# Attention with half-array scores and a three-step lead, and feed-forward stages with normalising on GpSimd and wide passes

## The reference

```python
def attend(q, k, v):                      # 16 heads of 16
    return softmax(q @ k.T / 4) @ v       # over 256 keys
x = x + lora_linear(attend(q(ln(x)), k(ctx), v(ctx)))   # W + 2 A B for q, k, v, o, with biases
x = x + sqrt((ln(x) @ cos(theta + tn))**2 + (ln(x) @ sin(phi + pn))**2)
x = x + linear(attend(rope(q(ln(x))), rope(k(ctx)), v(ctx)))
h = gelu(quant16(ln(x)) @ quant8(W_in) + b_in)          # 256 to 1024 features
x = x + quant16(h) @ quant8(W_out) + b_out
```

## Time and profile before

| What | Value |
|---|---|
| median of 3 runs | 2490.02 us (2481.99 to 2492.55) |
| span of the profiled execution | 2491.9 us; no other time of that execution is given |
| busy in the span | PE 78%, PE weight load 63%, DVE 70%, ACT 53%, POOL 32% |
| granted clock, mean | 0.880 |
| DMA | 333.54 MB, mean 134 GB/s |

### The profile page before, as it was taken

The page is one execution under the profiler, slowest core; times in us unless marked ns, Lnnn a source line. Parts: engine busy times, 40 slices in busy tenths (PEclk is TensorE's granted clock), DMA queues, the critical chain, the costliest instruction groups (busy, mean ns, idle before and its releaser), DMA issues. The chain is left out here.

```text
span 2491.9 us, 47293 instructions
## 1 busy us (share of the span) xinstructions
PE 1955.9 (78%) x14240; PEld 1576.1 (63%) x14240; DVE 1747.3 (70%) x3674; ACT 1316.8 (53%) x2381; POOL 797.0 (32%) x866
## 2 busy tenths in 40 slices
PE   1689999999999679277788777887777775786687
PEld 0567777777777467255666666666666663665676
DVE  6567778877877378465667767767666665676788
ACT  0255666656655378144444444444444443786676
POOL 3012222222222200423333333333333332221787
PEclk9899999999999689578888888888888877898899
DMA  5576887888878100356665656666666661356565
GB/s 164 107 157 145 169 172 162 166 169 166 170 161 165 53 3 0 76 104 122 123 120 116 117 109 116 119 112 118 111 118 122 121 118 54 135 220 252 196 242 186
DMA packets 259781, 333.54 MB, mean 134 GB/s; under 512 B 29152, under 2 KB 237184, under 8 KB 251520
## 3 DMA queue, kind: packets, MB, share of 16 engines
q1 hardware_dynamic: 233088, 277.00, 49.4%
q0 software_dynamic: 26624, 55.67, 9.6%
HBM read 185.70 MB, written 144.70 MB: 133 GB/s over the span
## 5 line engine op out<-in xcount | busy, mean ns | idle before, releaser
L610 DVE TENSOR_REDUCE L_negm<-L_s_bank 128x2 f32<-128x512 f32 x1024 | 684.4, 684 | 363.2 <-PE L_s_bank L418 360.7
L475 ACT ACTIVATE L_prob<-L_t_bank 128x512 f32<-128x512 f32 x1024 | 598.9, 598 | 631.8 <-PE L_t_bank L429 625.7
L418 PE MATMUL L_s_bank<-L_kst,L_qst 96*128 96x256 f32 x2048 | 526.1, 343 | 236.5 <-DMA L_kst<-k_scratch 176.7
L418 PEld LDWEIGHTS L_s_bank<-L_kst,L_qst 96*128 96x128 f32 x2048 | 355.4, 216 | 363.0 <-issue 142.0
L429 PE MATMUL L_t_bank<-L_qst,L_kst 98*128 98x256 f32 x2048 | 460.6, 311 | 18.3 <-ACT L_prob L475 15.2
L429 PEld LDWEIGHTS L_t_bank<-L_qst,L_kst 98*128 98x128 f32 x2048 | 361.7, 217 | 33.3 <-ACT L_prob L475 30.0
L339 PE MATMUL L_o_bank<-L_prob,L_vext 128*32 128x256 f32 x4096 | 301.1, 415 | 2.7 <-ACT L_prob L475 2.7
L1289 PE MATMUL G_acc<-G_w_out,G_hhl 128*128 128x256 f32 x1024 | 140.4, 291 | 59.4 <-DVE G_hhl L1259 59.1
L259 POOL DMA_DIRECT2D L_den<-o_scratch x64 | 35.5, 554 | 452.2 <-DMA o_scratch<-L_osb 452.2
L1289 PEld LDWEIGHTS G_acc<-G_w_out,G_hhl 128*128 128x128 f32 x1024 | 127.9, 192 | 72.1 <-DVE G_hhl L1259 37.5
L339 PEld LDWEIGHTS L_o_bank<-L_prob,L_vext 128*32 128x32 f32 x4096 | 112.5, 115 | 92.6 <-issue 18.8
(11 more groups left out here) (172 smaller groups left out, 3257.2 us busy)
## 6 DMA issues: line engine op xcount, KB each, us to landing
L_qst<-q_scratch SPq DMA_DIRECT2D x384, 128.0 KB, 5.0
L_kst<-k_scratch SPq DMA_DIRECT2D x384, 128.0 KB, 6.4
q_scratch<-L_qhl SPq DMA_DIRECT2D x64, 512.0 KB, 3.0
k_scratch<-L_khl SPq DMA_DIRECT2D x64, 512.0 KB, 3.2
o_scratch<-L_osb POOLq DMA_DIRECT2D x128, 256.0 KB, 4.8
hidden_scratch<-G_hid SPq DMA_DIRECT2D x32, 1024.0 KB, 3.9
G_hid<-hidden_scratch SPq DMA_DIRECT2D x32, 1024.0 KB, 7.4
L_ctx_in<-in_ctx SPq DMA_DIRECT2D x64, 256.0 KB, 3.2
```

Source lines behind the costliest of these rows:

```text
L418: mm = pe.matmul(s_bank[k % 2][:, j, :], qst[1 - q][0:96, h, P * qt:P * (qt + 1)], kst[1 - q][0:96, h, :], start=True, stop=True)
L475: act.activation(prob[g % 2][:, k % 2, 2 * (k // 2 % 2):2 * (k // 2 % 2) + 2, :], t_bank[k % 2][:, :, :], ACT.Exp, scale=HD ** -0.5).then_ ...
L610: dve.tensor_reduce(negm[:, t, 2 * pair:2 * pair + 2, qt], s_bank[k % 2][:, :, :], AX.X, ALU.max, negate=True).then_inc(sem["dve_s"], 1)
```

## The change

In both attentions a head's stack has 48 rows (50 with the maxima) and lies in rows 0 to 49 or 64 to 113. A slot holds one head position of both feature halves; the half of the rows alternates with the batch, so that the scores of batch i+1 and the transposed scores of batch i lie in opposite halves, and their four matmuls are issued in turn. A batch is normalised by GpSimd and projected three steps before its exponentials (q, k) or two (v). ScalarE copies projections and values out of PSUM, GpSimd splits q and k; the rotation takes its swapped copy by DMA between partitions (`rotated`, two DMAs of 64 partitions) and is done by GpSimd (`times`, a product); q and k are stored in pieces of 4 KB and stacked in pieces of 2 KB. The bias of v is folded into that of the output. The context's split transpose is stored by layer 0 and loaded by layer 1. Outputs (`eo`, heads in 17 columns) stay in SBUF: denominators, `merge` and the spread of the reciprocals (`rb`) are DMAs on SP's queue, and GpSimd multiplies. `weighted(n, half)` is the product of exponentials and v for eight heads. The memsets of the stacks go.

In the feed-forward stages GpSimd normalises, and in `cos_sin_ffn` it also adds to x; maxima in `quantised_in` are taken over 1024 columns; `quantised_out` works on half chunks of 2048 columns, with three load buffers, and GpSimd and VectorE share the scaling back. All loops are written out. Below, added lines without their outer indent.

```diff
-    for c, part in enumerate(order):
-        sp.dma_start(dst[HD * c:HD * (c + 1), HT * t:HT * (t + 1), :].bitcast(F32),
-                     dram[part, t].rearrange("(h d) q -> d h q", d=HD)).then_inc(done, 16)
+def stack(n, half):
+    u = n % 2 ^ half
+    for st, dram, high in ((kst[n % 2], k_dram[n % 2], KH), (qst[n % 2], q_dram[n % 2], QH)):
+        part = dram.rearrange("(j d) c t q -> j d c (t q)", d=HD)[HJ * u:HJ * (u + 1)]
+        sp.dma_start(st[64 * u:64 * u + 2 * HD, :, :, :].bitcast(F32), part.rearrange("j d c n -> (d c) j n")).then_inc(sem[f"stack{half}"], 16)
+        sp.dma_start(st[64 * u + 2 * HD:64 * u + ROWS, :, :, :].bitcast(F32),
+                     part[:, :, high, :].rearrange("j d n -> d j n")).then_inc(sem[f"stack{half}"], 16)
...
+def step(i):
+    if on(i + 1):
+        after(sp, sem["pe_t"], 16 * i)
+        stack(i + 1, 1)
+    if on(i):
+        maxima(i, 1)
+    if on(i + 2):
+        after(sp, sem["stack1"], 64 * (i + 1))
+        sp.wait_ge(sem["pool_k"], i + 3)
+        store(khl, k_dram[i % 2], sem["k_store"])
+        sp.wait_ge(sem["pool_q"], i + 3)
+        store(qhl, q_dram[i % 2], sem["q_store"])
+    if on(i + 4):
+        if rope:
+            after(sp, sem["pe_v"], i + 3)
+            after(sp, sem["ctx_load"], 16 * (i + 4))
+        else:
+            sp.wait_ge(sem["pe_cT"], i + 4)
+        load_ctx(i + 4)
+    if on(i - 1):
+        sp.wait_ge(sem["act_eo"], i)
+        after(sp, sem["dve_rd"], i - 1)
+        for u in range(2):
+            sp.dma_start(den[64 * u:64 * (u + 1), :], osb[HD:P:32, u, :, :]).then_inc(sem["den_load"], 16)
+    if on(i + 3) and not rope:
+        sp.wait_ge(sem["dve_cT"], i + 4)
+        sp.dma_start(c_dram[i + 3 - lo], cT[0][:, :, :, :].bitcast(F32)).then_inc(sem["c_store"], 16)
+    if on(i + 3) and rope:
+        sp.wait_ge(sem["act_kf"], i + 4)
+        rotated(kf, kr, sem["k_rot"])
+    if on(i - 1):
+        sp.wait_ge(sem["den_load"], 32 * i)
+        after(sp, sem["merge"], 64 * (i - 1))
+        for g in range(4):
+            sp.dma_start(osb[32 * g + HD:32 * (g + 1), 0, :, :], osb[32 * g:32 * g + HD, 1, :, :]).then_inc(sem["merge"], 16)
+    if on(i + 2):
+        sp.wait_ge(sem["k_store"], 32 * (i + 3))
+        sp.wait_ge(sem["q_store"], 32 * (i + 3))
+        after(sp, sem["pe_t"], 16 * i + 8)
+        stack(i + 2, 0)
+    if on(i - 1):
+        sp.wait_ge(sem["dve_rd"], i)
+        after(sp, sem["r_load"], 16 * (i - 1))
+        for u in range(2):
+            sp.dma_start(r_dram.rearrange("(g c n) -> c g n", g=4, c=2)[u], rden[64 * u:64 * (u + 1), :]).then_inc(sem["r_store"], 16)
+    if on(i + 3) and rope:
+        sp.wait_ge(sem["act_qf"], i + 4)
+        rotated(qf, qr, sem["q_rot"])
+    if on(i + 1):
+        maxima(i + 1, 0)
+    if on(i - 1):
+        sp.wait_ge(sem["r_store"], 32 * i)
+        after(sp, sem["pool_y"], i - 1)
+        sp.dma_start(rb[:, :, :], r_dram.rearrange("(h a n) -> h a n", h=8, a=1).to_broadcast([8, HD, KT * S])).then_inc(sem["r_load"], 16)
...
+def step(i):
+    n = i + 3
+    if rope and on(i + 2):
+        low(i + 2, qhl, qf, QH, sem["act_qh"], sem["pool_q"])
+    if on(i - 2):
+        pool.wait_ge(sem["act_y"], i - 1)
+        pool.tensor_tensor(yhl[:, 1, :, :], yT[:, :, :], yhl[:, 0, :, :].bitcast(F32), ALU.subtract).then_inc(sem["pool_yl"], 1)
+    if on(n + 1):
+        normalise(n + 1)
+    if on(n):
+        add_bias(n)
+        if rope:
+            times(kr[:, :, :], 1, sem["k_rot"], 32 * (n - lo + 1))
+            times(kf, 0, sem["k_rot"], 32 * (n - lo + 1))
+            pool.wait_ge(sem["pool_r"], 4 * (n - lo) + 2)
+            pool.tensor_tensor(kf, kf, kr[:, :, :], ALU.add).then_inc(sem["pool_kh"], 1)
+            times(qr[:, :, :], 1, sem["q_rot"], 32 * (n - lo + 1))
+            times(qf, 0, sem["q_rot"], 32 * (n - lo + 1))
+            pool.wait_ge(sem["pool_r"], 4 * (n - lo) + 4)
+            pool.tensor_tensor(qf, qf, qr[:, :, :], ALU.add).then_inc(sem["pool_qh"], 1)
+            low(n, khl, kf, KH, sem["act_kh"], sem["pool_k"])
+        else:
+            split(n, khl, kf, KH, sem["act_kf"], sem["pool_kh"], sem["pool_k"])
+            split(n, qhl, qf, QH, sem["act_qf"], sem["pool_qh"], sem["pool_q"])
+    if on(i - 1):
+        pool.wait_ge(sem["r_load"], 16 * i)
+        pool.wait_ge(sem["merge"], 64 * i)
+        after(pool, sem["pool_yl"], i - 1)
+        pool.tensor_tensor(yT[:, :, :], osb[:, 0, :, :], rb[:, :, :], ALU.mult).then_inc(sem["pool_y"], 1)
...
+def scores(n, k):
+    half, j, qt = k // 8, k % 8 // 2, k % 2
+    u = n % 2 ^ half
+    if k % 8 == 0:
+        pe.wait_ge(sem[f"stack{half}"], 64 * (n + 1))
+    after(pe, sem["dve_s"], 16 * n + k - 1)
+    rows = slice(64 * u, 64 * u + ROWS)
+    for t in range(KT):
+        mm = pe.matmul(s_bank[k % 2][:, t, :], qst[n % 2][rows, j, t, P * qt:P * (qt + 1)], kst[n % 2][rows, j, t, :],
+                       start=True, stop=True)
+        if t == KT - 1:
+            mm.then_inc(sem["pe_s"], 1)
+        yield
...
+def step(i):
+    n = i + 3
+    for k in range(16):
+        first = scores(i + 1, k) if on(i + 1) else iter(())
+        second = scores_T(i, k) if on(i) else iter(())
+        for _ in range(KT):
+            next(first, None)
+            next(second, None)
+        if k == 2:
+            if on(i):
+                after(pe, sem["dve_mT"], 2 * i + 1)
+                maxima(i, 1)
+            if on(i + 2):
+                after(pe, sem["act_kf"], i + 3)
+                after(pe, sem["dve_x"], i - 2)
+                if rope:
+                    pe.wait_ge(sem["ctx_load"], 16 * (i + 3))
+                project_rows(m1, cT[(i + 2) % len(cT)], whl["v"]).then_inc(sem["pe_v"], 1)
+            if on(i - 1):
+                weighted(i - 1, 1)
+        if k == 4 and on(n):
+            pe.wait_ge(sem["pool_xn"], n + 1)
+            after(pe, sem["dve_mT"], 2 * i + 2)
+            after(pe, sem["act_qf"], n)
             transposes(m0, xn).then_inc(sem["pe_xT"], 1)
+            after(pe, sem["act_v"], n)
+            pe.wait_ge(sem["ctx_load"], 16 * (n + 1))
+            if rope:
+                project(m1, whl["k"], cT[n % 2]).then_inc(sem["pe_k"], 1)
+            else:
+                transposes(m1, ctx_in).then_inc(sem["pe_cT"], 1)
+        if k == 6 and on(n):
+            pe.wait_ge(sem["dve_xT"], n + 1)
             project(m0, whl["q"], xT).then_inc(sem["pe_q"], 1)
+        if k == 7 and on(n) and not rope:
+            pe.wait_ge(sem["dve_cT"], n + 1)
+            project(m1, whl["k"], cT[0]).then_inc(sem["pe_k"], 1)
+        if k == 10:
+            if on(i - 2):
+                pe.wait_ge(sem["pool_yl"], i - 1)
+                after(pe, sem["act_kf"], min(n + 1, hi))
+                after(pe, sem["act_v"], min(i + 3, hi))
                 after(pe, sem["dve_x"], i - 2)
+                project_rows(m1, yhl, whl["o"]).then_inc(sem["pe_o"], 1)
+            if on(i + 1):
+                after(pe, sem["act_qf"], min(n + 1, hi))
+                maxima(i + 1, 0)
+            if on(i):
+                weighted(i, 0)
...
+def step(i):
+    n = i + 3
     for k in range(16):
+        if on(i):
+            half, j, kt = k // 8, k % 8 // 2, k % 2
+            act.wait_ge(sem["pe_t"], 16 * i + k + 1)
+            if k % 8 == 0:
+                after(act, sem["pe_pv"], 2 * i + half - 1)
+            act.activation(prob[half][:, kt, j, :, :], t_bank[k % 2][:, :, :], ACT.Exp, scale=HD ** -0.5).then_inc(sem["act_p"], 1)
+        if k == 1 and on(i + 2) and rope:
+            act.wait_ge(sem["pool_qh"], i + 3)
+            act.activation(qhl[:, QH, :, :], qf, ACT.Copy).then_inc(sem["act_qh"], 1)
+        if k == 2 and on(i - 2):
+            act.wait_ge(sem["pool_y"], i - 1)
             after(act, sem["pe_o"], i - 2)
+            act.activation(yhl[:, 0, :, :], yT[:, :, :], ACT.Copy).then_inc(sem["act_y"], 1)
+        if k == 3 and on(i + 2):
+            act.wait_ge(sem["pe_v"], i + 3)
+            after(act, sem["pe_pv"], 2 * i)
+            act.activation(vext[(i + 2) % 3][:, :, :].rearrange("p t (h s) -> p t h s", s=VS)[:, :, :, 0:HD],
+                           m1[:, :, :].rearrange("p t (h d) -> p t h d", d=HD), ACT.Copy).then_inc(sem["act_v"], 1)
+        if k == 4 and on(i - 1):
+            act.wait_ge(sem["pe_pv"], 2 * i)
+            after(act, sem["pool_y"], i - 1)
+            act.activation(osb[:, :, :, :], eo[:, :, :, :], ACT.Copy).then_inc(sem["act_eo"], 1)
+        if k == 5 and on(n):
+            act.wait_ge(sem["pe_xT"], n + 1)
+            after(act, sem["pe_q"], n)
             act.activation(xT[:, 0, :, :], m0[:, :, :], ACT.Copy).then_inc(sem["act_xT"], 1)
+        if k == 6 and on(n) and not rope:
+            act.wait_ge(sem["pe_cT"], n + 1)
+            after(act, sem["pe_v"], n)
+            after(act, sem["pe_k"], n)
+            after(act, sem["c_store"], 16 * n)
+            act.activation(cT[0][:, 0, :, :], m1[:, :, :], ACT.Copy).then_inc(sem["act_cT"], 1)
```

(91 more changed lines are left out.)

1067 lines of the change are left out of this document (363 added, 704 removed).

## The result

The changed kernel takes 2749.06 us (median; 2746.34 to 2750.48) against 2491.28 beside it: a ratio of 1.104, 95% interval 1.099 to 1.109, 10% slower. The forecast was 2426, with a range of 2140 to 2545. The profiled execution has a span of 2748.7 us, against 2491.9 before.

What follows compares the result with a forecast made beforehand. Attention bounds it, by waits through two-deep score banks and two TensorE blocks. Terms: first attention +141 -5, second -160 -10, cosine +5, input -16, output -19, sum -64; 2490 - 64 = 2426 us, range 2140 to 2545.

Steps and rivals of the forecast that it cites:

- Rival B: Attentions: engine sums decide, as the banks cover more; steps near 21 and 24.5 us, 2135 us in all; chance 0.18.
- Step "the clock": Both attentions: half the TensorE block behind slot 2 runs at 1.2 GHz, 1.8 us more, steps of 27.1 and 27.5.
- (f): Both attentions: slot 2 and its block (projection v, product of half 1, transposed maxima), 3.8 us.
- (e): VectorE's tail, slots 11 to 15 and 0 of the next step: 7.1 us in the first attention, 8.4 second.
- (a): From slot 3's start, ScalarE's exponentials and copies and VectorE's low part before projection q: 5.25 us first attention, 5.75 second.
- (c): From slot 7 or 8, ScalarE's two exponentials and a copy before projection o: 2.5 us first attention, 2.75 second.
- Rival C: Attentions: clock falls in both blocks, half arrays not free side by side; steps 29.0 and 29.2, 2541 us; chance 0.23.
- (d): Both attentions: projection o, transposed maxima and the weighted product of half 0 on TensorE, 3.55 us.
- rival D: Second attention: GpSimd's list, with products at 1.79 us, bounds it; a step of 30 us, 2506 us; chance 0.09.
- Output -19: Rounded output stage: a chunk falls from 10.8 to 9.4 us, -22, with +3 for the coarser start and end.
- Input -16: Rounded input stage: normalising leaves ScalarE, wide maxima are hidden, a chunk falls from 9.6 to 8.6 us: -16 us.
- Cosine and sine +5: Cosine and sine stage: TensorE keeps 3.3 us a batch, GpSimd gets 2.7 to 3.2; +5 us, bound 0 to +10.

Runs made afterwards that it cites:

- filled run: The changed kernel with the four matmuls of a slot issued three times over in ten of sixteen slots: 2736 us, against 2749.
- last run: Changed kernel with blocks broken up, stores on GpSimd's queue, SP's list reordered, old cosine stage, y copied at slot 10 in the first attention: 2287 us.
- two edits: Each against the changed kernel (2749 us): stores of q and k on GpSimd's queue, 2577 us; TensorE's blocks broken up over the slots, 2585 us; both, 2657 us.

## Why the prediction was wrong

**What bounds the kernel, and the mechanism: right.** The steps sit on a chain through two-deep banks and two blocks; five joints of twelve came within 0.3 us. VectorE waits behind slots 2 and 10 with TensorE as the releaser, 5.8 and 5.5 us where I had said 3. Rival B, by engine sums, is out.

**Step "the clock", 1.8 us a step: mis-sized.** I let half of block (f) run slow. In the first attention projections k, o, v and both weighted products do. In the step shown k takes 2.69 us from its start to the next, o 2.2, v 2.8, the products 2.6 and 3.2, slots 7 and 2 0.73 and 0.77. At full clock a projection takes 1.6 there, a product 1.85, such a slot 0.43. The difference is 5.7 us in that step and 5.4 in the mean of the first attention, 4.1 in the second: this is the failed step of the first attention. I had looked for lulls in (e) alone; (a) and (c) are lulls as well. In the step shown, 5.7 less the 1.8 allowed, with 0.8 of the next term, less the 1.1 by which (a) and (e) came out shorter than forecast, are the 3.6 that it lies over 27.1. The mean step is 1.1 shorter than this one, which leaves a miss of 2.5 us a step, 80 us. The filled run took 4.2 us of these 5.4 away, and bears the size out by the pieces' lengths, though not by its time. How the 5 us that breaking up gave divide between the clock, the consumers' waiting and TensorE's longer work stays open.

**Durations of TensorE's pieces: mis-sized.** I took 1.43 for a projection, 0.24 for a slot and 2.0 for a product. The slot holds between neighbours of its own kind; between full-array pieces it takes 0.43. Projections take 1.6 at full clock, o 1.5, and a product 1.85. In the kernel before, 1.43 was k's alone; q, v and o took 1.53. There a slot between two projections took no more than one between slots, 0.48 us:

```profile
414.97 0.40 PE L418 MATMUL L_s_bank<-L_kst,L_qst 96*128 96x256 f32 x2
...
415.45 1.60 PE L324 MATMUL L_m<-L_wv,L_cT 128*128 128x256 f32 x12
```

So I put the added 0.2 us down to the change between full-array and half-array matmuls, which is new with the change. Timeline of the last run, with q's two halves at full clock:

```profile
504.31 0.98 PE L361 MATMUL L_m<-L_xT,L_wq 128*128 128x256 f32 x6
505.22 0.39 PE L381 MATMUL L_s_bank<-L_kst,L_qst 48*128 48x256 f32 x1
...
505.65 0.98 PE L361 MATMUL L_m<-L_xT,L_wq 128*128 128x256 f32 x6
```

A half takes 0.91 and a slot between the two 0.43, so breaking a projection up costs 0.2 us beside the slots. In the changed kernel the durations add little: three projections by 0.2, o by 0.1, two slots by 0.2, less 0.3 for the products, some 0.8 us a step. Rival C had this as a drain of up to 1.6 us a step, which is of the right size, and I had set it aside because no wait was shown. The Trainium skill, "TensorEngine Tiling (Array Packing)", "Key Properties", says that a change of tiling mode drains the engine and that different tiles run in parallel; the trace agrees with both, at 0.2 us for a slot.

**Step (c) in the second attention, 2.75 us: the step that failed.** I wrote that the stall of the present step goes because stores and stacks lie beside a whole step. The readers' wait did go; no score matmul waits for keys in the changed kernel. But a buffer that is stored must be empty before its next writer, and I never asked when the writer comes. The stores stand behind the second maxima on SP, and are issued at 1812.80 and 1815.27; the writers come at slots 6 and 7. (c) took 7.4 us for 2.75, so that is 4.7 us a step, and the stores' move gave back 4.8. I priced SP by issues "near 0.4" each, against readers only; the stores of 4 KB pieces take 0.6 to 1.8 us each, the copies between partitions 0.6. With the clock's share (1.8 in (d) and 1.7 in (f), less the 1.8 allowed) this is 6.4 of the 6.9 us that the step shown is over the forecast of 27.5. The difference by stage was missed by 22 us more through my base: 32.5 is the step of 1200 to 1900 us, and the whole attention has 31.8.

**GpSimd's list (rival D): not the bound.** The products that I feared at 1.79 take 1.27 to 1.28. Working beside GpSimd did show on VectorE: the 128x16 casts and differences take 421 and 322 ns in the second attention, 175 and 176 in the first, 0.8 us a step or 25 us in all. The Trainium skill, "SBUF — State Buffer", "Who interferes with whom", says that a VectorE copy in the two-port mode and GpSimd block each other for a whole instruction, and that a VectorE instruction with two SBUF inputs contends with a GpSimd one that reads SBUF; the trace agrees. The largest in the step above is a difference of two inputs, 1.19 us, nearly as long as a GpSimd pass of 1.27.

**The other stages.** Output -19: measured -23, in part by luck. A chunk takes 132.2 / 14 = 9.4 us in the mean as said, but five chunks take 8.4 each and the others some 10.0, in which ScalarE waits 2.2 to 2.4 us a chunk for a load; nothing in my sum has these two lengths. Input -16: wrong, +3. I had ScalarE as the bound and called the wide maxima hidden; they stand in VectorE's list ahead of the second low part, for which TensorE waits at each chunk's start. Putting the low part first brought 0.3 us a chunk, not the 1.2 missed, so the next wait stands close behind. Cosine and sine +5: +14, past my bound of +10. TensorE needs 3.2 us a batch and does not keep it. By the trace the first four batches run at 3.2, and 3.65 begins where GpSimd's sum does. In ScalarE's in-order list the root of one batch (at 1160.41) stands ahead of its squares and the copy of `xT`, on which VectorE's low part and its sum (at 1163.08) wait, and the next root (at 1164.05) waits for them; the sum takes 0.94 us beside GpSimd and 0.68 without. No run tried this cause.

**Chances.** Rival C was the nearest, for the reason that it gives (clock in both blocks), but its 2541 lies 208 us under the result, since it had neither the writers' wait nor the slow key projection. I had given it 0.23, and 0.28 to any slower time. A sum of two steps of 63.0 against its 56.6 decides.

## What to carry to other kernels

When a transfer moves a wait off its reader, ask the same of its writer: when is the buffer wanted again, and what stands before the store in its queue. An in-order list that also waits must be sorted by when its results are needed, each time that anything it waits for is moved: here two edits, each worth 6%, gave 3% together and 14% once SP's list was sorted, with some other moves beside it. Two long blocks of TensorE work cost twice over, once in the consumers' idle time and once in the clock that the lulls before them leave. Breaking them up has a price too: here some 4 us a step of TensorE's time by my estimate, since full-array and half-array work then alternate in every slot. And a kernel whose time is a chain should be summed from what each piece takes at its place, since a slot took 0.23 or 0.43 us by its neighbours.

## What the hardware showed that I had not expected

The row halves of the array take their matmuls apart from the order of issue: issued as score, score, transposed, transposed, they still start in pairs 0.01 us apart. The same pairs cost 0.23 us a slot next to their own kind and 0.43 between full-array pieces; the full-array scores of the kernel before took 0.48 at either place. The clock fell after a lull had ended: in the step of the changed kernel shown above TensorE was busy 0.93 of the 2 us from 922, still at a granted clock of 1.00, and it was the projection starting at 926.28 that ran at 0.50. Tiny VectorE passes of 0.18 us took up to 1.19 us beside GpSimd.
